# More softmax blocks per phase on VectorE, with its passes interleaved, in a one-core decoder layer

## The reference, cut to what matters

```python
qh = _split_heads(q @ Wq + bq)
kh = _split_heads(k @ Wk + bk)
vh = _split_heads(v @ Wv + bv)
logits = jnp.einsum('bhsd,bhtd->bhst', qh, kh) / jnp.sqrt(jnp.asarray(DEPTH, qh.dtype))
attn = jax.nn.softmax(logits, axis=-1)
out = jnp.einsum('bhst,bhtd->bhsd', attn, vh)
```

## Time and profile before

| what | us |
|---|---|
| median of 3 runs | 834.01 |
| the runs | 833.79 to 841.13 |
| the profiled execution | 833.03 |
| its span | 831.3 |
| ACT busy | 736.0 |
| PE busy | 707.7 |
| DVE busy | 689.5 |

### The profile page before, as it was taken

How to read it: one execution, slowest core, us unless ns; L and a number is a source line. 1 busy time by engine, 2 the same in 40 slices (tenths; PEclk the granted TensorE clock), 3 DMA queues, 4 the chain that set the end, 5 groups by cost and what they waited for, 6 DMA issues and landing times.

```text
span 831.3 us, 38425 instructions
## 1 busy us (share of the span) xinstructions
PE 707.7 (85%) x15210; PEld 319.9 (38%) x15212; DVE 689.5 (83%) x1952; ACT 736.0 (89%) x650; POOL 174.9 (21%) x304
## 2 busy tenths in 40 slices
PE   6996679899899998899998999888899998899841
PEld 3445434443444344334443444344433443344321
DVE  3518767996999699969996999699978997899766
ACT  2436879999999999999999999999999999999741
POOL 2501511221222122212221222122212221222100
PEclk9998989999999999999999999999999999999965
DMA  3303521111111111111111111111111111111000
GB/s 105 83 25 107 170 86 37 37 43 44 38 36 45 42 37 38 43 43 38 36 44 43 36 37 40 44 38 35 40 48 35 37 37 49 37 36 38 14 1 26
DMA packets 36611, 38.41 MB, mean 46 GB/s; under 512 B 8430, under 2 KB 35088, under 8 KB 36512
## 3 DMA queue, kind: packets, MB, share of 16 engines
q1 hardware_dynamic: 35644, 36.59, 14.8%
q10 hardware_dynamic: 868, 0.48, 0.2%
HBM read 30.15 MB, written 6.42 MB: 44 GB/s over the span
## 4 chain that ended last, share of the span: by engine, by line
ACT 40%; issue 24%; PE 16%; SPq 10%; DVE 5%; DMA 3%; POOL 1%; ACTq 1%; POOLq 0%; DVEq 0%
ACT probs L710 39%; SPq L291 8%; PE ps L1314 6%; PE ps L1284 3%; PE ps L1213 2%; PE ps L1199 2%; DMA k_op<-k_parts_dram 2%; SPq L505 1%; DMA k_parts_dram<-k_parts 1%; PE ps L1162 1%; DVE stats L776 1%; PE ps L1449 1%; ACTq L723 1%; POOL k_parts L541 0%; DMA q_parts_dram<-q_parts 0%
## 5 line engine op out<-in xcount | busy, mean ns | idle before, releaser
L710 ACT ACTIVATE probs<-ps 128x1536 f32<-128x1536 f32 (+1 forms) x536 | 671.7, 1379 | 11.9 <-PE ps L1284 11.4
L1314 PE MATMUL ps<-probs,v_op 64*9 64x512 f32 (+1 forms) x8384 | 523.5, 494 | 13.8 <-DMA k_op<-k_parts_dram 9.1
L1284 PE MATMUL ps<-q_op,k_op 59*32 59x512 bf16 x6432 | 337.4, 382 | 60.7 <-ACT probs L710 56.4
L979 DVE SCALAR_TENSOR_TENSOR e_u<-e_u,e_f 128x256 f32<-128x256 f32 x720 | 259.2, 425 | 0.0
L1284 PEld LDWEIGHTS ps<-q_op,k_op 59*32 59x32 bf16 x6432 | 107.9, 90 | 331.5 <-issue 245.7
L1314 PEld LDWEIGHTS ps<-probs,v_op 64*9 64x9 f32 x8384 | 169.3, 86 | 90.2 <-issue 27.7
L588 POOL TENSOR_SCALAR e_pow<-e_t 128x512 int32<-128x512 int16 x120 | 74.4, 620 | 353.9 <-DVE e_t L960 353.9
L960 DVE TENSOR_SCALAR e_t<-ps 128x256 f32<-128x256 f32 x240 | 90.5, 418 | 60.5 <-PE ps L1284 51.3
L581 POOL COPY v_op<-v_all 128x108 f32<-128x108 f32 x136 | 68.3, 502 | 181.3 <-PE ps L1314 180.6
L979 DVE SCALAR_TENSOR_TENSOR e_u<-e_f 128x256 f32<-128x256 f32 x240 | 90.1, 416 | 0.2
L986 DVE SCALAR_TENSOR_TENSOR probs<-e_u,e_pow 128x256 f32<-128x256 f32 x240 | 89.6, 411 | 0.0
(11 more groups left out here) (177 smaller groups left out, 257.7 us busy)
## 6 DMA issues: line engine op xcount, KB each, us to landing
k_op<-k_parts_dram SPq DMA_DIRECT2D x544, 36.0 KB
k_parts_dram<-k_parts SPq DMA_DIRECT2D x17, 288.0 KB, 2.5
k_op<-k_parts_dram SPq DMA_DIRECT2D x272, 12.0 KB
ctx_nat<-in_ctx_dram SPq DMA_DIRECT2D x16, 192.0 KB, 2.6
q_op<-q_parts_dram SPq DMA_DIRECT2D x32, 48.0 KB
q_parts_dram<-q_parts SPq DMA_DIRECT2D x2, 384.0 KB, 3.4
x_nat<-in_x_dram SPq DMA_DIRECT2D x1, 512.0 KB, 3.9
o_t<-att_rows SPq DMA_DIRECT2D x28, 16.0 KB
```

What stands on the lines that cost most here:

```text
L710: act.activation(probs[:, b % NP].rearrange("p u t -> p (u t)")[:, 0:columns], ps[:, bank:bank + BU, :].rearrange("p u t -> p (u t)")[:, 0 ...
L979: dve.scalar_tensor_tensor(out=e_u[:, cols], in0=u[:, cols], scalar=a, in1=e_f[:, cols], op0=ALU.add, op1=ALU.mult).then_inc(e_step, 1)
L1284: return pe.matmul(ps[a:a + P // G, bank, :], k_op[W2 * r:W2 * r + KR, kslot, i, P * j + a:P * j + a + P // G], q_op[W2 * r:W2 * r + KR, q ...
L1314: last = pe.matmul(ps[32 * k:32 * k + DH + 1, ACC[h], a:b], v_op[W2 * h:W2 * h + W2, slot, j, (DH + 1) * k:(DH + 1) * (k + 1)], probs[W2 * ...
```

## The change

VectorE takes 19 units per phase in place of 15: block (0, 0), five in every four chunks from chunk 2 to 13 (blocks (0, 2), (1, 1), (2, 0), (2, 3), (3, 2) of the four), and (14, 2), (15, 1), (16, 0). By the number of the block these are 0, 10, 13, 16, 19, 22, 26, ... 54, 58, 61 and 64, so the distance from one to the next is 3 blocks, 4 after every fifth, and 10 at the start of a phase.

A unit is now two passes over the scores in halves, as before, and four passes of 512 columns: a square, a cube, a scaling with e_pow and a product (a polynomial of degree 4 in two factors). e_f, e_u and e_pow have two buffers. The scaling and the product of a unit are issued between the passes of the next unit: e_t, e_t, e_f, e_f, scale of the one before, square, finish of the one before, cube. Only the first unit of a phase is finished at once.

The values of a chunk come two steps later than before, and its four steps are now: the second half of j = 1 and then j = 2 of the chunk two back, j = 0 and then the first half of j = 1 of the chunk before. Each step's matmuls go by row halves, the half first that the last score matmul of the step doesn't use. At the start of a phase four such steps of full width follow each other. Loops of ScalarE now hold 4 chunks (were 2). The last chunks' values are made behind the last block.

```diff
-E_BLOCK = BPC - 2
-E_UNITS = NC - 2
-EXP2_LEAD = 0x3aae0400
-EXP2 = [753.2197875976562, 522.0919799804688, 180.93934631347656,
-        41.8090705871582, 7.287810325622559]
+E_LOOP = 4
+E_TURN = ((0, 2), (1, 1), (2, 0), (2, 3), (3, 2))
+E_FIRST = 2
+E_AT = ([(0, 0)] + [(c + k, t) for c in range(E_FIRST, NC - 3, E_LOOP) for k, t in E_TURN] +
+        [(NC - 3, 2), (NC - 2, 1), (NC - 1, 0)])
+E_UNITS = len(E_AT)
+EXP2_OFF = 2
+EXP2_LEAD = 0x3a8bec00 - EXP2_OFF * 2 ** 23
+EXP2 = [9.525652885437012, 28.199888229370117, 45.54460906982422, 132.23011779785156]
 E_MIN = -116.0
-E_STEPS = 12
-E_TAKEN = 4
+E_AHEAD = 1
...
+        qf, qr = q_work[:, 0:2, :], q_work[:, 2:4, :]
+        e_f = [e_f0[:], q_work[:, 0, :]]
+        e_u = [e_u0[:], q_work[:, 1, :]]
+        e_pow = [e_pow0[:], q_work[:, 2, :].bitcast(I32)]
...
-        def e_count(ph, c):
-            return ph * E_UNITS + max(c - 1, 0) + 1
...
+            return ph * E_UNITS + sum(at <= (c, t) for at in E_AT)
         def e_low(ap):
...
-            def powers(ph, c):
-                pool.wait_ge(e_step, E_STEPS * (e_count(ph, c) - 1) + 2)
-                pool.tensor_scalar(e_pow[:], e_low(e_t[:]), float(2 ** 23), float(EXP2_LEAD),
+            def powers(ph, c, t):
+                n = e_count(ph, c, t)
+                pow2 = e_pow[n % 2]
+                if n > 2:
+                    pool.wait_ge(e_probs, E_AHEAD + n - 2)
+                pool.wait_ge(e_rounded, 2 * n)
+                pool.tensor_scalar(pow2, e_low(e_t[:]), float(2 ** 23), float(EXP2_LEAD),
                                    ALU.mult, ALU.add).then_inc(e_pow_ready, 1)
             for ph in range(PHASES):
                 for c in range(NC):
                     m = ph * NC + c
-                    stage(m % 2, m, c * CT, ph % NG * G)
-                    if c != 1 and c < NC - 1:
-                        powers(ph, c)
+                    for t in range(BPC):
+                        if t == 2:
+                            stage(m % 2, m, c * CT, ph % NG * G)
+                        if (c, t) in E_AT:
+                            powers(ph, c, t)
...
+            def chunk(ph, c, i=None):
+                f = ph * BPP + c * BPC
+                for t in range(LAST_BPC if c == NC - 1 else BPC):
+                    count = f + t + 1 + AHEAD
+                    exponentials(f + t, count if i is None else i * (E_LOOP * BPC) + count,
+                                 BU * 512 - EW if (c, t) in E_AT else BU * 512)
...
+            e_done = [0]
+            e_marks = {}
+            def mark(n, name):
+                e_done[0] += 1
+                e_marks[n, name] = e_done[0]
+            def make_probs(ph, at, before):
+                def score(block):
+                    return ps[:, BU * (block % 2) + BU - 1, :]
+                n = e_count(ph, *at)
+                block = ph * BPP + at[0] * BPC + at[1]
+                f, u = e_f[n % 2], e_u[n % 2]
+                if n > 1:
+                    dve.wait_ge(e_pow_ready, n - 1)
                 dve.wait_ge(scores_done, block + 1 + AHEAD)
                 for cols in halves:
...
+                    dve.tensor_scalar(e_t[:, cols], score(block)[:, cols], E_MIN, ROUND + EXP2_OFF,
+                                      ALU.max, ALU.add).then_inc(e_rounded, 1)
+                for i, cols in enumerate(halves):
+                    dve.wait_ge(e_rounded, 2 * (n - 1) + i + 1)
+                    dve.scalar_tensor_tensor(out=f[:, cols], in0=score(block)[:, cols], scalar=E_MIN,
                                              in1=e_low(e_t[:, cols]), op0=ALU.max, op1=ALU.subtract
...
+                                             ).then_inc(e_taken, 1)
+                if before:
+                    scale(*before)
+                dve.wait_ge(e_taken, 2 * n)
+                dve.scalar_tensor_tensor(out=u, in0=f, scalar=EXP2[0], in1=f, op0=ALU.add, op1=ALU.mult
+                                         ).then_inc(e_step, 1)
+                mark(n, "square")
+                if before:
+                    finish(*before)
+                dve.wait_ge(e_step, e_marks[n, "square"])
+                dve.scalar_tensor_tensor(out=f, in0=u, scalar=EXP2[2], in1=f, op0=ALU.add, op1=ALU.mult
+                                         ).then_inc(e_step, 1)
+                mark(n, "cube")
+            def scale(ph, at):
+                n = e_count(ph, *at)
+                f = e_f[n % 2]
+                dve.wait_ge(e_pow_ready, n)
+                dve.wait_ge(e_step, e_marks[n, "cube"])
+                dve.scalar_tensor_tensor(out=f, in0=f, scalar=EXP2[3], in1=e_pow[n % 2].bitcast(F32),
+                                         op0=ALU.add, op1=ALU.mult).then_inc(e_step, 1)
+                mark(n, "scaled")
+            def finish(ph, at):
+                n = e_count(ph, *at)
+                block = ph * BPP + at[0] * BPC + at[1]
+                dve.wait_ge(e_step, e_marks[n, "scaled"])
+                dve.scalar_tensor_tensor(out=probs[:, block % NP, BU - 1, :], in0=e_u[n % 2],
+                                         scalar=EXP2[1], in1=e_f[n % 2], op0=ALU.add, op1=ALU.mult
+                                         ).then_inc(e_probs, 1)
...
+                for n, at in enumerate(E_AT):
+                    make_probs(ph, at, (ph, E_AT[n - 1]) if n > 1 else
+                               (ph - 1, E_AT[-1]) if ph and n == 0 else None)
+                    if n == 0:
+                        scale(ph, at)
+                        finish(ph, at)
+                        if ph:
+                            add_acc(ph - 1)
+                            turn_acc()
+                            if ph > 1:
+                                dve.wait_ge(o_written, 16 * G * (ph - 1))
+                            dve.transpose(att_rows[:], acc_t[:].rearrange("p n d -> p (n d)")
+                                          ).then_inc(att_ready, 1)
+            scale(PHASES - 1, E_AT[-1])
+            finish(PHASES - 1, E_AT[-1])
...
-            def values(slot, first_block, j, last_chunk, count=1, first=False, a=0, b=HQ):
+            def values(slot, first_block, j, last_chunk, lead, count=1, first=False, a=0, b=HQ):
                 packed = last_chunk and j == CT - 1
-                for k in range(G):
-                    block, u = divmod(j * G + (0 if packed else k), BU)
-                    for h in range(R2):
+                for h in (lead, 1 - lead):
+                    for k in range(G):
+                        block, u = divmod(j * G + (0 if packed else k), BU)
                         if packed and h != k // G2:
...
+                def wait_unit(signal, ahead, each, ph_u, c_u, t):
+                    turn = 0 if i is None else 1
+                    if (c_u + turn * E_LOOP, t) in E_AT:
+                        n = e_count(ph_u, c_u + turn * E_LOOP, t) - turn * len(E_TURN)
+                        wait(signal, at(ahead + each * n, each * len(E_TURN)))
+                def made(back, j, a=0, b=HQ, count=1, first=False):
+                    ph_v, c_v = (ph, c - back) if c >= back else (ph - 1, c - back + NC)
+                    if ph_v < 0:
+                        return
+                    if j == 0:
+                        wait(v_staged, at(m - back + 1, KS))
+                    if a == 0:
+                        for t in range(BPC):
+                            if (t * BU + BU - 1) // G == j:
+                                wait_unit(e_probs, E_AHEAD, 1, ph_v, c_v, t)
+                    values((m - back) % 2, ph_v * BPP + c_v * BPC, j, c_v == NC - 1, 1 - s % 2,
+                           count, first, a, b)
                 for s in range(LAST_BPC if c == NC - 1 else BPC):
...
+                    if c or s >= 2:
+                        wait_unit(e_taken, 0, 2, ph, *((c, s - 2) if s >= 2 else (c - 1, s + 2)))
+                    elif ph:
+                        wait_unit(e_taken, 0, 2, ph - 1, NC - 1, s + 1)
+                    wait(probs_ready, at(f + s + 1, KS * BPC))
                     scores(m % KS, q, ph, c == NC - 1, s)
                     if s == 2 and m + 1 < PHASES * NC:
...
+                        wait(k_loaded[(m + 1) % KS], at(K_LOAD * ((m + 1) // KS + 1), K_LOAD))
                     if c == 0:
...
+                        if s < 2:
+                            made(2, s + 1, count=2 - s)
+                        else:
+                            made(1, s - 2, count=s - 1)
+                    elif c == 1 and s < 2:
+                        if s == 0:
+                            made(2, 2)
                     elif s == 0:
+                        made(2, 1, a=HQ // 2)
+                    elif s == 1:
+                        made(2, 2)
+                    elif s == 2:
                         if c == 1 and ph:
                             pe.wait_ge(acc_step, ACC_STEPS * (ph - 1) + 2)
...
+                        made(1, 0, first=c == 1)
                     else:
```

(9 more changed lines are left out.)

99 lines of the change are left out of this document (18 added, 81 removed).

## The result

The changed kernel takes 846.38 us (median of 4 runs, 845.04 to 848.56), the kernel before 833.91 in the same runs. The ratio is 1.0138, 95% interval 1.0093 to 1.0184. The profiled execution is the 845.04 us one.

What follows compares the result with a forecast made beforehand. The prediction took ScalarE to bound the kernel, with almost no slack. From 833.0 us profiled, -12.8 + 11.8 + 6.7 + 1.0 gave 839.7, and with part of the copies' cost 840.5 us; 8-in-10 range 824 to 852.

Steps and rivals of the forecast that it cites:

- What the change gives ScalarE: ScalarE: 4 more short blocks a phase, 32 in all, each worth 0.40 us, together -12.8 us.
- VectorE's unit: VectorE: a 512-column pass takes 0.60 us, a unit 3.74 (3.46 to 4.22), which fits beside ScalarE's work.
- Inside a phase: TensorE's value steps wait 0.3 to 0.45 us for finished units, making ScalarE late by 1.5 a phase: +11.8 us.
- At a phase's start: Values wait 1.5 us for unit (16, 0), ScalarE stalls 1.1; 1.4 a phase against today's 0.4: +6.7 us.
- Behind the last block: After the last block: two context tiles of chunk 15 join the values, VectorE's last unit ends: +1.0 us (0 to 2).
- Row halves: TensorE's value matmuls: it already starts on the free half of the array, so ordering by row halves is worth 0.
- the fourth rival: TensorE runs in program order, so the new order gives back at most 8 us: 832 us; chance 0.03.
- SyncE's queue: At a phase's start: o_t's DMAs and the loads of k_op keep their places in SP's queue; no time charged.
- My case: Late waits take ScalarE's gain back, 833 to 848 us; chance 0.50.
- the first: Rival: the waits cost ScalarE nothing and its saving arrives, 827 us, or 820 without the phase-start wait; chance 0.23.
- The second: Rival: VectorE becomes the bound, 852 us at a pass of 0.62, 870 at 0.65; chance 0.20.
- The third: Rival: scores come late, a ScalarE short block costs 1.05 us, the gain is 9, not 12.8: 844 us; chance 0.04.

Runs made afterwards that it cites:

- Experiment 2: The changed kernel with GpSimd making e_pow for half of its 512 columns only, part of the computation left out: 839.46 us, ratio 1.0043 against the kernel before.
- experiment 4: The changed kernel with four units in every four chunks, all in block 2, 16 units a phase: 841.41 us, ratio 1.0067 against the kernel before.
- experiment 12: `late_turn` with the scaling pass left out and SyncE's loop over a phase's middle chunks written out: 815.15 us, ratio 0.9765 against the kernel before.
- `late_turn`: The changed kernel with values one step later and a turn's five units at (0, 2), (1, 1), (2, 0), (3, 0), (3, 3): 836.65 us, ratio 0.9988.
- `late`: The changed kernel with its 19 units where they are and the values one step later: 838.87 us, ratio 1.0012 against the kernel before.
- experiment 3: The changed kernel with 18 units, without (16, 0), and (15, 1) finished at once: 837.48 us, ratio 1.0032 against the kernel before.
- experiment 1: The changed kernel with value matmuls in the old order, head by head, both row halves in turn: 847.66 us, ratio 1.018 against the kernel before.
- experiment 9: The changed kernel with VectorE's scaling pass left out, part of the computation missing: 835.09 us, ratio 0.9992 against the kernel before.
- experiment 10: `late_turn` with VectorE's scaling pass left out, part of the computation missing: 834.85 us, ratio 0.9996 against the kernel before.

## Why the prediction was right, and where not

I said 840.5 us (824 to 852) because late waits would take the saving back. The time fell in the range, 5.9 above the forecast: the kernel became slower by 12.5 us where I had 6.5. Step by step:

- **What the change gives ScalarE**: -12.8. Measured are 1.7 a phase or -13.7 where nothing is late, and -12.6 with the 0.94 that a short block takes with its usual 0.035 of waiting. Held.
- **VectorE's unit**: 0.60 for a 512-column pass. The square, finish and cube passes start 0.602 before the next. Held. But back to back a unit is 3.78 to 3.86 us, not 3.74, for the step failed that let **e_pow** cost nothing. I had read it from the pair at 403.27, which lay beside only the last 0.13 us of the e_pow at 402.78. The scaling pass has 0.65, and the passes that meet a copy 0.677. The Trainium skill ("SBUF — State Buffer", Who interferes with whom) had said that both contend; the trace agrees, at 0.05 and 0.075 us a pass, where I had charged 0.08 to one and nothing to the other. Experiment 2 prices it at 0.9 us a phase, 7 us of the total: without it the time is 839.5, close to my forecast.
- **Inside a phase**: +11.8 (1.5 a phase), in three places of 0.26 to 0.43 and four of 0.12 (these add up to 1.6, not 1.5, which is 1 us of the total). Measured are eleven of 0.13 to 0.27 and three small ones, 2.85; counted as I counted, with a short block at 0.94, about 2.4. The mechanism was half right. Beside the values' wait for a finished unit stands the scores' wait for the unit's reads, which I had found too and dismissed ("the wait by itself costs ScalarE nothing"). Two terms of that were too small. With units of 3.8 us three blocks (3.57) apart VectorE's lag grows: in settled phases its last read ends a median of 0.41 after ScalarE's. And I let TensorE start 0.14 after the read, the time that values take behind `add_acc`, but inside TensorE's loop over chunks the scores start 0.34 after it (0.05 to 0.10 outside the loop). My own rows had this number: the short activation ends at 402.34 + 1.05 = 403.39, and the scores two blocks on start at 403.74, 0.35 later. With it six late blocks a phase, 1.3 us together, follow by arithmetic: with A the start of a short activation, ScalarE wants the scores at A + 0.905 + 1.334 = A + 2.24. They take 0.61 and the activation starts 0.04 behind them, so they must start by A + 1.6. Those at 389.48 start at A + 1.86 (A is 387.62), and the activation is late by 0.27. The other late blocks inside a phase stand behind value steps that start late, and how the two waits share them no run separates. Experiments 2, 4, and 12 against `late_turn` show that VectorE's pace is behind them, and `late`, that the values' wait alone isn't.
- **At a phase's start**: 1.4 a phase, a wait of 1.5 with ScalarE idle for 1.1. Measured 1.75, a wait of 1.37, idle 1.16. The mechanism is shown by experiment 3; the further 0.48 is behind block 0, where I had 0.3.
- **Behind the last block**: +1.0 (0 to 2), measured +2.6. The values of chunk 15 now follow the product of the last unit but one, (15, 1), instead of lying beside the last blocks, and the last values start 4.2 us after the last activation's start, where they had started 1.6 after it:

```profile
793.20 1.93 PE L1357 MATMUL ps<-probs,v_op 64*9 64x512 f32 x32 [0.44 <-DVE probs L1027]
...
796.15 2.77 PE L1357 MATMUL ps<-probs,v_op 64*9 64x512 f32 x40
```

- **Row halves**: 0. Held (experiment 1), to 0.2 us a phase. Of the fourth rival its delay falls: no value step begins 0.2 later in the old order. My reason, that TensorE starts on the free half, isn't shown, since most steps keep the order of the program.
- **SyncE's queue**: "the loads of k_op keep their places in SP's queue". They do, but this sentence is the largest thing I missed. I looked for what the change moves past the queue and not at how full it was. The phases of 85 us at the end of the kernel before were the sign, and so were the two lines of its page; I carried the phases over as unexplained excess. After the change phases of 86.2 are longer than the queue's, so that excess is swallowed: 3.5 us in phases 4 to 6 (+3.5 where phases 1 to 3 have +7.0). It hid part of my error inside a phase.

From my 839.7 to the 845.0 of the profiled execution are 5.3 us: inside a phase 8 x 0.9 = +7.2, phase starts 7 x 0.35 = +2.5, the tail +1.6, the swallowed queue waits -3.5, and phase 0, which became 2.0 shorter where a settled phase became 2.2 longer, -4.2. That is +3.6; 1.7 are spread over phases and not assigned. In phase 0 TensorE waits once for `k_op`, 3.99 us before and 0.54 after. That is some 3.5 of the 4.2; why the wait was shorter wasn't tested, and in other kernels' traces it is anything from 0.5 to 4.4.

That the time fell in the range is in part luck. I had foreseen neither the swallowed queue waits nor the shorter phase 0; without these 7.7 us the late waits, as they were, would have given some 854. The sign "a phase of 84.5" was also lower than my own terms give (83.9 - 1.6 + 1.5 + 1.0 = 84.8); measured were 86.2.

Of the rivals the first could not have come true at all: with nearly every late block gone the queue still holds the kernel at some 835 us, as experiments 9 and 10 show. I gave it 0.23. The second had the right kind of mechanism, VectorE's length, and its price was of the right size: with (0.65 + 3 x 0.602)/4 = 0.614 and the copies a mean pass is some 0.62, for which it had 852, and a hundredth of a pass costs 5.5 us by experiment 2 (0.05 a unit, 0.0125 a pass, 6.9 us) where it had 6. My case and this rival were parts of one mechanism. The third is nearer to the trace than its 0.04: short blocks are 0.905 where VectorE is not behind, but a settled phase has seven of 19 over 1.0, and their mean is 1.02, where this rival had 1.05. It names the same late scores from ScalarE's side.

## What to carry to other kernels

Before pricing a saving on the bounding engine, read the queue that issues the transfers as an engine of its own: how long it takes for one stage's transfers, and whether it ever waits; if it hardly does, that time is a floor for the stage, and only a lead hides it. Late phases that are longer than early ones with the same work are the sign of a lead running out. Units placed closer together than one takes need their average and also the lag that they build up; a cost of 0.05 us on a pass is worth nothing by itself and nearly 1% of the kernel when it repeats in such a run. Take the time from a release to the start behind it from the same pair of instructions, in the same loop: 0.14 and 0.34 us decided here whether a wait cost nothing.

## What was unexpected of the hardware

- Issuing a transfer holds SyncE's queue for a time that differs by its shape: 24 rows of 1.5 KB take some 0.7 us, 8 rows 0.31 in the loop and 0.46 with constant addresses. Rows alone don't give it: the o_t transfers of 8 rows of 2 KB take 0.63 to 0.70. A chunk's six loads take 15.56/4 = 3.9 us with constant addresses and (61.57 - 3.9)/12 = 4.8 in the loop, where register instructions precede each one.
- Behind VectorE's last read of a unit, TensorE's scores start 0.34 us later inside its loop over chunks and 0.05 to 0.10 later outside it (trace of the changed kernel).
- A VectorE pass over PSUM and SBUF beside e_pow kept its 0.41 us; one over two SBUF operands grew from 0.68 to 0.73, and beside a 128 x 108 copy to 0.755.
